# The values of the second attention as two full-array products, with ScalarE's copies sorting the heads, and new orders on every engine

## The reference, cut to what matters

```
x = x + tanh(g_xattn[0]) * performer(layernorm(x), ctx, ctx, random_features)       # causal, exp features
x = x + tanh(g_ffn[0])   * channel_mix(layernorm(x), W_r, W_k, W_v, mu_r, mu_k)
x = x + tanh(g_xattn[1]) * attention2(ctx, layernorm(x), w_kv, w_q, w_la, w_proj, b_proj, att_weight)
x = x + tanh(g_ffn[1])   * quantised_ffn(layernorm(x), w_gate, w_up, w_down)

# attention2, per sequence: 16 heads of 8 numbers
k, v = split(ctx @ w_kv)                      # keys and values of the context
a    = softmax(q k^T / sqrt(8))
a2   = softmax(gate * a)                      # gate: mean and max over the sequence of ctx @ w_la
out  = (att_weight * a2 + (1 - att_weight) * a) @ v @ w_proj + b_proj
```

## Time and profile before

| what | us |
|---|---|
| median of 3 runs | 500.12 (500.04 to 507.09) |
| profiled execution, its own time | 502.34 |
| its span, first to last instruction | 500.4 |
| PE busy | 447.7 (89%) |
| DVE busy | 407.0 (81%) |
| ACT busy | 348.2 (70%) |
| POOL busy | 341.4 (68%) |

### The profile page before, as it was taken

The page is one execution under the profiler, slowest core; times in us unless marked ns, Lnnn a source line. Parts: engine busy times, 40 slices in busy tenths (PEclk is TensorE's granted clock), DMA queues, the critical chain, the costliest instruction groups (busy, mean ns, idle before and its releaser), DMA issues.

```text
span 500.4 us, 18610 instructions
## 1 busy us (share of the span) xinstructions
PE 447.7 (89%) x7642; PEld 329.6 (66%) x7670; DVE 407.0 (81%) x1208; ACT 348.2 (70%) x735; POOL 341.4 (68%) x548
## 2 busy tenths in 40 slices
PE   3698989899999999879899999999999999888887
PEld 3157767586758677666667666767777776665776
DVE  6577648677989899865989799889889899899785
ACT  2342547766888787845688778878788877786663
POOL 6115355778786886854876969685979877787821
PEclk9979999999999999975999999999999999999999
DMA  6821101012101120020011110101100000000000
GB/s 187 216 66 30 48 22 36 22 37 59 37 25 29 33 56 8 18 65 24 21 42 35 36 30 26 40 22 29 35 2 19 3 19 8 13 17 1 12 12 24
DMA packets 33013, 18.28 MB, mean 37 GB/s; under 512 B 5281, under 2 KB 32801, under 8 KB 32929
## 3 DMA queue, kind: packets, MB, share of 16 engines
q1 hardware_dynamic: 32352, 17.07, 13.0%
q10 hardware_dynamic: 576, 0.02, 0.1%
HBM read 9.74 MB, written 2.10 MB: 24 GB/s over the span
## 4 chain that ended last, share of the span: by engine, by line
PE 35%; POOL 23%; DVE 20%; ACT 9%; issue 5%; DMA 4%; SPq 3%; POOLq 0%; ACTq 0%; DVEq 0%
PE MC L1579 6%; POOL call L421 5%; PE TP L1556 5%; POOL call L439 3%; POOL ft L378 3%; PE SP L1547 3%; PE FP L1472 2%; PE MA L1501 2%; PE FP L1476 2%; DVE WT L1030 2%; DVE mx L1073 2%; SPq L251 2%; DMA call<-in_ctx 2%; DVE call L1084 2%; POOL kX L384 2%
## 5 line engine op out<-in xcount | busy, mean ns | idle before, releaser
L1556 PE MATMUL TP<-ident,call 128*128 128x128 f32 x512 | 77.5, 283 | 3.8 <-POOL call L439 2.0
L1579 PEld LDWEIGHTS MC<-Vc,ET 128*64 128x64 f32 x2048 | 65.9, 139 | 16.9 <-issue 9.4
L1579 PE MATMUL MC<-Vc,ET 128*64 128x25 f32 x2048 | 72.2, 219 | 3.2 <-DVE X L1225 1.6
L1556 PEld LDWEIGHTS TP<-ident,call 128*128 128x128 f32 x512 | 56.8, 143 | 24.7 <-issue 10.2
L378 POOL TENSOR_SCALAR ft<-ft 128x512 f32<-128x512 f32 x64 | 39.8, 621 | 32.4 <-ACT ft L614 27.9
L439 POOL TENSOR_TENSOR call<-call,Gs 128x1024 f32<-128x1024 f32 x32 | 60.9, 1902 | 1.2
L421 POOL TENSOR_TENSOR call<-call,rsh 128x1024 f32<-128x1024 f32 x32 | 60.9, 1902 | 0.6
L679 ACT ACTIVATE ET<-TP 128x512 f32<-128x512 f32 x64 | 37.0, 594 | 16.9 <-PE TP L1556 16.6
L1073 DVE TENSOR_REDUCE mx<-SP 128x16 f32<-128x1024 f32 x32 | 38.9, 1215 | 11.2 <-PE SP L1547 11.2
L1030 DVE TENSOR_TENSOR WT<-FP,mask 128x512 f32<-128x512 f32 x64 | 42.0, 678 | 3.4 <-PE FP L1489 3.3
L666 ACT ACTIVATE ET<-TP 128x512 f32<-128x512 f32 x64 | 37.1, 595 | 10.3 <-PE TP L1556 10.1
(11 more groups left out here) (219 smaller groups left out, 1100.6 us busy)
## 6 DMA issues: line engine op xcount, KB each, us to landing
Cd<-in_ctx SPq DMA_DIRECT2D x32, 128.0 KB, 2.8
call<-in_ctx SPq DMA_DIRECT2D x4, 512.0 KB, 7.9
xall<-in_x SPq DMA_DIRECT2D x4, 512.0 KB, 4.4
cz<-cT SPq DMA_DIRECT2D x64, 32.0 KB, 1.8
cz<-csq SPq DMA_DIRECT2D x64, 32.0 KB, 1.9
kX<-kT SPq DMA_DIRECT2D x128, 8.0 KB
out_x<-X SPq DMA_DIRECT2D x16, 128.0 KB, 2.0
ffn<-in_L_ffn_w_gate SPq DMA_DIRECT2D x1, 256.0 KB, 4.6
```

Source lines behind the costliest of these rows:

```text
L1556: last = pe.transpose(TP[:, c:c + P], src[:, c:c + P], ident[:, :])
L1579: last = mm(MC[64 * j:64 * j + 64, c + 32 * q:c + 32 * q + 25], weights[:, q, 64 * j:64 * j + 64], Vc[g.p][:, 2 * u + j, q, 0:25], start=T ...
```

## The change

`values` makes two products on the full array for the values, one for each pair of sequences: 128 context rows stationary, the 128 unsorted columns of the value weights moving. Both halves of the heads now come out on the same partitions, and the two sequences of a pair on different halves. `values1` on ACT therefore makes four copies of 64 partitions by 128 numbers instead of two of 64 by 256; two of them read one half of the partitions and write the other. `Wv2`, ACT's two copies that made it and PE's wait for them are gone. A few waits that another one implies are dropped, and a few are added. The tables of all five engines are written anew; PE's has 359 products of zeros instead of 401.

```diff
-            act.wait_ge(s("wk_in"), 48)
-            for h in range(2):
-                act.activation(Wv2[:, h, :], wkv[:, P:2 * P].rearrange("c (q h d) -> c h q d", q=8, h=2)[:, h], ACT.Copy)\
-                    .then_inc(s("wv2"), 1)
...
             def values1(g):
 
+                at(act, s("oB"), g.k * 2 - 2)
                 at(act, s("pKV"), g.k + 1)
                 for h in range(2):
-                    act.activation(Vc[g.p][64 * h:64 * h + 64, :, :, 16 * h:16 * h + 8],
-                                   FP[64 * h:64 * h + 64, 768:1024].rearrange("p (b q d) -> p b q d", b=4, q=8),
-                                   ACT.Copy).then_inc(s("Vc"), 1)
+                    for j in range(2):
+                        act.activation(Vc[g.p][64 * h:64 * h + 64, j::2, :, 16 * h:16 * h + 8],
+                                       FP[64 * j:64 * j + 64, 768:1024].rearrange("p (b q h d) -> p h b q d", b=2, q=8, h=2)[:, h],
+                                       ACT.Copy).then_inc(s("Vc"), 1)
...
             def values(g):
                 mm(FP[:, 512:768], wkv[:, 0:P], cT[:, 256 * g.k:256 * g.k + 256], start=True, stop=True)
-                for b in range(4):
-                    for h in range(2):
-                        last = mm(FP[64 * h:64 * h + 64, 768 + 64 * b:768 + 64 * b + 64],
-                                  cT[:, 256 * g.k + 64 * b:256 * g.k + 64 * b + 64], Wv2[:, h, :], start=True, stop=True)
+                for b in range(2):
+                    last = mm(FP[:, 768 + P * b:768 + P * b + P], cT[:, 256 * g.k + P * b:256 * g.k + P * b + P], wkv[:, P:2 * P],
+                              start=True, stop=True)
                 last.then_inc(s("pKV"), 1)
...
# SP's table, two of eight lines
-            load(G[8]); store(G[0]); strips(G[9]); store(G[1]); load(G[9]); spread(G[5]); spread(G[6])
-            strips(G[10]); rows(3); store(G[2]); load(G[10]); spread(G[7]); strips(G[11]); store(G[3])
+            strips(G[8]); load(G[8]); spread(G[5]); store(G[1]); strips(G[9]); spread(G[6]); load(G[9])
+            load(G[10]); store(G[2]); rows(3); strips(G[10]); spread(G[7]); store(G[3]); load(G[11])
```

More of the change, by code:

```diff
@@ new lines, in _ @@
+            pe.wait_ge(s("F"), 15); project_T(G[2]); turn1(G[3], 3)
+            pe.wait_ge(s("hh"), 3); ffn_gu(G[1], 1); out0(G[5], 0)
+            pe.wait_ge(s("n1"), 7); outA(G[3], 1); out0(G[5], 1); features(G[6], 0)
+            pe.wait_ge(s("n1"), 8); ffn_dn(G[0], 1); rows_CT(G[4]); turn2(G[3], 0); turn2(G[3], 1)
+            pe.wait_ge(s("out"), 2); project(G[2])
+            pe.wait_ge(s("fe"), 26); features(G[6], 1)
+            pe.wait_ge(s("S"), 13); ffn_down(G[1], 0); queries(G[4])
@@ new lines, in _ @@
+            pe.wait_ge(s("X3"), 4); outB(G[4], 0)
+            pe.wait_ge(s("hg"), 6); rows_CT(G[5]); turn2(G[4], 2); queries(G[5]); turn2(G[4], 3)
+            pe.wait_ge(s("hh"), 6); scores(G[5], 0); rows_BT(G[6]); rows_T(G[8]); values(G[6])
+            pe.wait_ge(s("n2"), 9); outB(G[4], 1); ffn0_in(G[6]); ffn_down(G[2], 0)
+            pe.wait_ge(s("Vc"), 28); weights0(G[7], 0)
+            pe.wait_ge(s("ls"), 11); scores(G[5], 1)
+            pe.wait_ge(s("n2"), 10); ffn_dn(G[2], 0); ffn_down(G[2], 1)
@@ new lines, in _ @@
+            pe.wait_ge(s("n2"), 12); ffn_dn(G[3], 1); ffn_gu(G[4], 0)
+            pe.wait_ge(s("thR"), 8); ffn0_out(G[7])
+            pe.wait_ge(s("out"), 8); outA(G[6], 0); turn1(G[6], 2)
+            pe.wait_ge(s("WT"), 34); weights0(G[8], 1); turn1(G[6], 3)
+            pe.wait_ge(s("F"), 27); project_T(G[5])
+            pe.wait_ge(s("hh"), 9); ffn_gu(G[4], 1)
+            pe.wait_ge(s("n1"), 13); outA(G[6], 1); out0(G[8], 0); out0(G[8], 1); features(G[9], 0)
+            pe.wait_ge(s("oT"), 6); turn2(G[6], 0)
@@ new lines, in _ @@
+            ffn0_in(G[10]); weights0(G[11], 0)
+            pe.wait_ge(s("S"), 35); ffn_down(G[6], 0)
+            pe.wait_ge(s("ls"), 19); scores(G[9], 1)
+            pe.wait_ge(s("n2"), 17); ffn_dn(G[6], 0); ffn_down(G[6], 1)
+            pe.wait_ge(s("WT"), 46); values(G[10])
+            pe.wait_ge(s("out"), 13); outB(G[8], 1)
+            pe.wait_ge(s("hT"), 14); ffn_in(G[7]); ffn0_out(G[10]); zeros(6, TP, 1)
+            pe.wait_ge(s("Vc"), 44); weights0(G[11], 1)
+            pe.wait_ge(s("xqT"), 8); turn1(G[9], 0); turn1(G[9], 1)
@@ new lines, in _ @@
+            turn2(G[9], 1)
+            pe.wait_ge(s("hh"), 16); scores(G[10], 0)
+            pe.wait_ge(s("n1"), 20); outB(G[9], 0); ffn0_in(G[11]); turn2(G[9], 2); turn2(G[9], 3)
+            pe.wait_ge(s("qT"), 14); weights0(G[12], 0)
+            pe.wait_ge(s("n2"), 19); outB(G[9], 1); scores(G[10], 1); ffn0_out(G[11]); ffn_down(G[7], 0)
+            pe.wait_ge(s("WT"), 50); values(G[11]); ffn_dn(G[7], 0); ffn_down(G[7], 1)
+            pe.wait_ge(s("vr"), 12); out0(G[12], 0)
+            pe.wait_ge(s("Vc"), 48); weights0(G[12], 1)
@@ new lines, in _ @@
+            pe.wait_ge(s("n1"), 26); project(G[11]); turn2(G[12], 1); queries(G[13])
+            pe.wait_ge(s("S"), 49); turn2(G[12], 2)
+            pe.wait_ge(s("X3"), 12); outB(G[12], 0); turn2(G[12], 3); scores(G[13], 0)
+            pe.wait_ge(s("fe"), 62); features(G[15], 1); rows_BT(G[14]); ffn_down(G[10], 0); outB(G[12], 1)
+            pe.wait_ge(s("ls"), 27); scores(G[13], 1)
+            pe.wait_ge(s("hT"), 21); ffn_down(G[10], 1); values(G[14])
+            pe.wait_ge(s("hT"), 22); project_T(G[12]); ffn_dn(G[10], 0); ffn0_in(G[14])
@@ new lines, in _ @@
+            pe.wait_ge(s("out"), 21); ffn_dn(G[10], 1)
+            pe.wait_ge(s("Vc"), 60); weights0(G[15], 0)
+            pe.wait_ge(s("oT"), 13); ffn_in(G[11]); ffn0_out(G[14])
+            pe.wait_ge(s("xqT"), 12); turn1(G[13], 0); turn1(G[13], 1)
+            pe.wait_ge(s("WT"), 62); weights0(G[15], 1); ffn_gu(G[11], 0); project(G[12])
+            pe.wait_ge(s("vr"), 15); out0(G[15], 0); out0(G[15], 1)
+            pe.wait_ge(s("X3"), 13); outA(G[13], 0)
+            pe.wait_ge(s("hh"), 23); ffn_gu(G[11], 1); turn1(G[13], 2); turn1(G[13], 3); values(G[15])
```

1133 lines of the change are left out of this document (527 added, 606 removed).

## The result

The kernel of the change takes 479.52 us (median of 4 runs, 477.89 to 480.57) against 500.67 us for the kernel before beside it. The ratio is 0.9551, with a 95% interval of 0.9479 to 0.9623: 21.2 us less, where the prediction had 12.5 and a range that ended at 480.0. The direction was right, the size was not. Medians are over all runs of a kernel, ratios leave out the runs that were in a slower state. The profiled execution of after has an own time of 478.8 us and a span of 477.0.

A forecast was written before the change was run, and what follows sets the result against it. The prediction took PE's own list as the bound, DVE close behind. Terms −1.1 + 1.5 − 8.5 − 1.4 − 3.0 = −12.5 took the profiled 502.34 us to 489.8, so 487.6 us in timed runs; range 480 to 499.

The forecast's parts named there:

- What bounds the kernel: Whole kernel: PE's own list is the bound, busy 94% and 93% in two long windows, with DVE close behind.
- the disturbance: From 208 to 240 us of before: two holes in PE's work, granted clock down to 0.86, then 0.66.
- the start: First groups: key masks, rounding and factors moved back bring the first mask 3.7 us earlier; −3.0 us taken, with zero products gone.
- the two long windows: 100 to 208 and 240 to 470 us of before, with PE busy 101.73 of 108.00 and 213.46 of 230.00 us.
- The last input rows: Their DMA goes ahead of group 10's strips; DVE's wait, PE's 1.72 us hole and the low clock go: −8.5 us.
- The first hole: PE's 1.15 us wait of `ffn_dn` for DVE before 211.41, with 1.7 us of clock loss; half taken, −1.4 us.
- the two moves: At the start: POOL's key masks behind the constants (2.5 us), DVE's rounding and factors behind the first mask (1.7 us).
- The products: `values` on PE: two full products take 0.55 us against 0.62 for eight small ones, −1.1 us over 16 groups.
- the copies: Four `Vc` copies on ACT for two: 5.0 us more work, exposed where `weights0` follows `values`; +1.5 us taken.
- A new hole in place of the old one: Rival: a new PE hole costs 8.5 us, giving 496.1 us, two give 504.6; chance 0.27 for one or two.
- No effect: Rival: DVE waits for the input rows as before, PE's list takes up the start's gain; about 500 us, chance 0.11.
- The copies' holes: Rival: `weights0` waits for `Vc` copies in nine groups, 2.9 us a hole, 26 us in all; 513.7 us, chance 0.06.

The follow-up runs named there:

- more_pe: The kernel after with the keys' product of `values` issued twice in every group, 6.9 us of PE work added in all: 482.50 us, 3.0 over after.
- before_rows_first: The kernel before with only the DMA of the last input rows moved ahead of the strips of group 10: 495.72 us, ratio 0.9871.
- before_3q: New products, last input rows first; order of before for what before starts in its first 374 us, then the new order: 498.59 us.
- after_start: New products, last input rows first; new order for what after starts in its first 62 us, then the order of before: 496.29 us.
- after_late_start: The kernel after with POOL's first two key masks back between the constants, DVE's third rounding and factors back ahead of the first group's work: 488.24 us.
- before_early_start: before_rows_first with POOL's first two key masks behind the constants, DVE's third rounding and factors behind the first group's work: 496.81 us, ratio 0.9928.
- old_products_new_orders: The kernel after with the eight small products, two copies a group and Wv2 of the kernel before: 479.48 us, ratio 0.9561.

## Why the prediction was right and wrong, point by point

- **What bounds the kernel.** Here the prediction failed. It read 93 to 94% of PE's time as busy, concluded that PE's own list is the bound, and so put what the new orders do outside the disturbance and the start at nothing, but for 1.7 us of its range. more_pe shows 43% where that claim wants all of it, and 10.0 of the 23.1 us lie in stretches for which the sum has no term. By the matched windows 7.1 us of that are idle time of PE that other orders of the same work leave out, around 250 to 300 in short waits for DVE, ACT and POOL; the rest is busy time of PE, and its cause is open. The trace of before had both signs: PE stands idle for 6.3 and 16.5 us in the two long windows, and the page's part 4 gives PE 35%.
- **The last input rows, −8.5.** Right in cause and size. Moved alone it gives 8.3 us by the traces and 6.5 by the ratio (4.4 to 8.5 by the interval). In after the DMA is issued 0.16 us after its place is free, where up to 3.1 us were allowed for, and DVE comes to the statistics 12.6 us after the end of attA (203.39 to 215.94), where 14.5 were worked out.
- **The first hole, −1.4.** It was given half of 1.15 + 1.7. In after the hole is gone altogether. The price was partly wrong: the same hole stands in before_rows_first, 1.18 us, without a fall of the clock, so the 1.7 us of clock loss did not follow from this hole alone. Where the clock does fall behind it with the rows first, in before_3q (0.88 from 208 to 220), the lead made from 175-200 to 250-275 is 8.0 us against 8.4 in before_rows_first, so that fall cost about 0.4 there, not 1.7.
- **The start, −3.0.** The first `weights0` and the first mask in the timelines of PE and DVE of after; the `weights0` stands 1.24 us ahead of the earlier trace rows:

```profile
40.79 1.16 PE L1484 MATMUL FP<-ft 32*64 32x64 f32 x64 [0.80 <-POOL ft L377]
```
```profile
42.02 1.29 DVE L1028 TENSOR_TENSOR WT<-FP,mask 128x512 f32<-128x512 f32 x2 [0.73 <-PE FP L1484]
```

  DVE's first mask stands at 42.02, 2.9 us ahead where 3.7 were worked out, and at 100 us the mean lead is 2.6 us. The size fits, within the scatter of 1 us. That its gain might be eaten by the steady list is not borne out: after_start is 1.2 us ahead of before_rows_first in 100-125 and still 1.0 in 350-375, and in after_late_start a delay comes out at the end in full. But the size was in part luck: the two moves to which the prediction put it down gain nothing by themselves (before_early_start), so the 2.6 belong to the start's new order as a whole.
- **The products, −1.1, and the copies, +1.5.** As work both were sized rightly. The groups by line and shape of after, PE and ACT:

```profile
L1460 PE MATMUL FP<-wkv,cT 128*128 128x128 f32 x64 | 10.2, 284 | 0.0
...
L589 ACT ACTIVATE Vc<-FP 64x128 f32<-64x128 f32 x64 | 17.3, 271 | 2.2 <-PE MC L1575 0.7 <-PE FP L1460 0.3
```

  A copy takes 271 ns where 264 were expected, and ACT's 5.3 us more stand against 5.0; `values` takes 0.54 us in the median from the first value product to the next instruction, against 0.62 with the eight (from PE's timelines, 16 groups each). By the Trainium skill, ScalarE: Activation LUTs, section What ACT_TABLE_LOAD costs, the estimate in the prediction was 293 ns a copy and 200 ns in a row of them; the 271 ns lie between, and in a row of four the starts are 294 ns apart (median of 48, from ACT's timeline), so the 200 do not show. As time neither shows: old_products_new_orders equals after. The 1.5 us were charged for waits of `weights0` for `Vc`. The weight loads of `weights0` do wait for it in after, seven times and 2.1 us in all, but none of the waits of PE's products that the view lists (from 0.15 us up) between 60 and 440 us is for `Vc`.
- **The rivals.** A new hole in place of the old one: not seen, from 100 to 400 us no hole of PE in after is over 0.9 us. No effect: refuted for the orders, true for the products. The copies' holes: refuted, as above. (Its 22.7 us should read 22.5, from 487.6 to 510.1; it is eight holes either way.)
- **The sum.** Of the forecast's 12.5 us, 3.0 + 9.9 are there as 2.6 + 10.5, the net cost of 0.4 for products and copies is nothing, and 10.0 us were missing. The range ended at 480.0 because only 1.7 us were left for "waits that I cannot see shorten"; it should have had a part of the 22.8 us that PE stands idle in the two long windows.

## What to carry to other kernels

Where four engines are busy for 70 to 90% of the time and wait for one another in turn, as here, the busiest need not be the bound: see how the chain that ended last divides among them, lengthen each list by a known piece of work that nobody waits for, and see how much comes out at the end before a term is set to nothing. When all lists of such a kernel are written anew, sum the short waits of the busiest engine over the steady stretch and put a good part of them into the range, not only the one large hole. A delay or a lead that all the lists have taken on, an early one too, stays to the end, while work added to a single list shows only in part; and one part of a new order moved by itself can cost more than it gives.
